# A fused attention and ternary feed-forward layer: the values' scratch in another order, and a prologue with its steps at other places

## The reference

```
qkv = layernorm(x) @ w_qkv;  q, k, v in 16 heads of 32;  q = [q1, q2], k = [k1, k2]
a   = softmax(q1 k1^T / sqrt(32)) - lam * softmax(q2 k2^T / sqrt(32))
lam = exp(lambda_q1 . lambda_k1) - exp(lambda_q2 . lambda_k2) + 0.8
out = a @ v, divided by its rms over the 32 columns, * norm_w * 0.2
x   = x + (heads and rows laid out anew) @ wo
y   = layernorm(x);  h = y @ (ternary(w_fc) * scale)^T + gate * y @ v^T @ fast_b^T @ u^T
x   = x + (relu(h)^2) @ (ternary(w_proj) * scale)^T
```

## Time and profile before

| | |
|---|---|
| median of 3 runs | 3759.39 us |
| profiled execution, its own time | 3755.76 us |
| its span | 3754.0 us |
| PE, DVE, ACT, POOL busy | 99%, 84%, 74%, 16% |
| first score matmul | 101.33 us |
| mean granted clock of TensorE | 0.996 |

### The profile page before, as it was taken

One profiled execution on the slowest core, in us unless ns is written; L12 is line 12 of the kernel. 1 busy time (PEld: TensorE's weight loads), 2 busy tenths in 40 slices (PEclk: granted clock), 3 DMA queues, 4 the chain that ended last, 5 costly groups with the idle time before them and its releaser, 6 DMA issues.

```text
span 3754.0 us, 57605 instructions
## 1 busy us (share of the span) xinstructions
PE 3705.5 (99%) x21704; PEld 2053.0 (55%) x21704; DVE 3152.0 (84%) x2927; ACT 2796.3 (74%) x3629; POOL 584.1 (16%) x269
## 2 busy tenths in 40 slices
PE   7999999999999999999999999999999999999999
PEld 6444444444444444444444444444468888888887
DVE  6899999999999999999999999988865555555554
ACT  4798888888888888888888989888863333333333
POOL 0101101023434343223223201210010000000000
PEclk9999999999999999999999999999999999999999
DMA  7544444445444444554554444534340101010010
GB/s 239 134 102 105 103 105 105 102 100 111 102 99 104 107 106 99 112 115 102 110 114 112 100 100 103 133 82 114 77 152 23 45 23 46 23 46 23 29 40 23
DMA packets 255350, 344.56 MB, mean 92 GB/s; under 512 B 118000, under 2 KB 142576, under 8 KB 254000
## 3 DMA queue, kind: packets, MB, share of 16 engines
q1 hardware_dynamic: 251504, 324.43, 36.6%
q0 software_dynamic: 3392, 15.73, 1.3%
q10 hardware_dynamic: 128, 0.03, 0.0%
HBM read 198.55 MB, written 131.07 MB: 88 GB/s over the span
## 4 chain that ended last, share of the span: by engine, by line
PE 88%; DVE 7%; issue 3%; DMA 1%; ACT 1%; SPq 0%; ACTq 0%; DVEq 0%
PE ps L875 22%; PE ps L850 16%; PE ps L940 13%; PE ps L995 12%; PE ps L786 9%; DVE acc L1632 5%; PE ps L926 4%; PE ps L789 4%; PE ps L896 3%; PE ps L945 2%; PE ps L758 1%; PE ps L1031 1%; PE ps L909 1%; PE ps L1016 1%; ACT pr L1261 0%
## 5 line engine op out<-in xcount | busy, mean ns | idle before, releaser
L1261 ACT ACTIVATE pr<-ps 128x1024 f32<-128x1024 f32 x2048 | 1989.8, 1029 | 257.0 <-PE ps L850 249.5
L1632 DVE TENSOR_TENSOR acc<-acc,pr 128x2048 f32<-128x2048 f32 x768 | 1780.9, 2319 | 40.3 <-ACT pr L1261 10.5
L875 PE MATMUL ps<-pr,vst 128*32 128x512 f32 x8192 | 1010.5, 599 | 0.3 <-DMA vst<-v_scratch 0.3
L850 PE MATMUL ps<-qst,kst 50*128 50x512 f32 x4096 | 781.9, 457 | 9.3 <-ACT pr L1261 6.9
L850 PEld LDWEIGHTS ps<-qst,kst 50*128 50x128 f32 x4096 | 337.1, 184 | 655.1 <-ACT pr L1261 460.1
L875 PEld LDWEIGHTS ps<-pr,vst 128*32 128x32 f32 x8192 | 213.4, 109 | 447.0 <-issue 436.6
L1430 ACT ACTIVATE rb<-ps,scf 128x512 f32<-128x512 f32 x228 | 157.0, 689 | 352.9 <-PE ps L945 352.9
L995 PE MATMUL ps<-tP,hh_ 128*128 128x512 f32 x1024 | 400.3, 391 | 0.6 <-DVE hl_ L1836 0.6
L995 PE MATMUL ps<-tP,hl_ 128*128 128x512 f32 x1024 | 399.5, 390 | 0.0
L786 PE MATMUL ps<-xt,wqh 128*128 128x512 f32 x1024 | 376.8, 419 | 3.0 <-DVE xt L1521 3.0
L940 PE MATMUL ps<-yh,tT 128*128 128x512 f32 x896 | 351.2, 392 | 0.0
(11 more groups left out here) (177 smaller groups left out, 3790.0 us busy)
## 6 DMA issues: line engine op xcount, KB each, us to landing
qst<-q_scratch SPq DMA_DIRECT2D x128, 256.0 KB, 4.6
kst<-k_scratch SPq DMA_DIRECT2D x128, 256.0 KB, 7.0
q_scratch<-stg SPq DMA_DIRECT2D x112, 256.0 KB
k_scratch<-stg SPq DMA_DIRECT2D x112, 256.0 KB
qst<-q_scratch SPq DMA_DIRECT2D x128, 128.0 KB, 4.9
kst<-k_scratch SPq DMA_DIRECT2D x128, 128.0 KB, 7.7
vst<-v_scratch SPq DMA_DIRECT2D x128, 128.0 KB, 4.6
xr<-in_L_attn_x_dram SPq DMA_DIRECT2D x64, 256.0 KB
```

The lines of the kernel that those rows point to most:

```text
L850: ins = e.matmul(ps[:, 2 * c + hh, :], kst[rows, r, j, t * 128:(t + 1) * 128], qst[rows, r, j, c * 512:(c + 1) * 512], start=True, stop=True)
L875: ins = e.matmul(ps[32 * c4:32 * c4 + 32, 4 + j, :], vst[:, r, t, 32 * hh:32 * hh + 32], pr[:, sl, c, hh, :], start=(t == 0), stop=(t == 7 ...
L1261: e.activation(pr[:, sl, c, :, :], ps[:, 2 * c:2 * c + 2, :], ACT.Exp, scale=SCALE).then_inc(s_exp, 1)
L1632: e.tensor_tensor(acc[:, j, :], old, new, ALU.add).then_inc(s_add, 1)
```

## The change

- v_scratch is laid out [2, 128, 8, 8, 64] (row, row tile, pair, columns) instead of [2, 8, 128, 8, 64] (pair first): a store writes 128 rows of 512 numbers, a load reads 4 pieces of 64 numbers for each of 128 partitions.
- w_qkv is split in another order: ScalarE copies columns 0 to 1023 of each k first and the values' columns between its turns; VectorE takes the low part of columns 0 to 127 and 512 to 639 ahead of T = 0, then the values', then the rest. T = 0 and 1 need the first, T = 2 the second, T = 3 the third.
- UNIT_AT is (7, 10, 17, 20) instead of (7, 9, 11, 12). woh is made at T = 16 instead of 22, wol at T = 18 instead of behind the loop. All five statistics steps of chunk 2 stand at T = 14.
- Chunk 2 is issued at T = 8 instead of 10, chunk 3 in pair 0 behind load_qk(1) instead of at T = 22.
- sync_shift(0) is on SyncE ahead of T = 21's store instead of on ScalarE.

```diff
-UNIT_AT = (7, 9, 11, 12)
+UNIT_AT = (7, 10, 17, 20)
-    vsc = nc.dram_tensor("v_scratch", [2, NP, 128, 8, 64], F32, kind="Internal").ap()
+    vsc = nc.dram_tensor("v_scratch", [2, 128, 8, NP, 64], F32, kind="Internal").ap()
...
-            e.dma_start(vsc[b % 2, :, :, t, :].rearrange("q p d -> p q d"),
-                        stage_v(V).rearrange("p (q d) -> p q d", q=NP)).then_inc(s_vsg[V % 2], 16)
+            e.dma_start(vsc[b % 2, :, t].rearrange("p q d -> p (q d)"), stage_v(V)).then_inc(s_vsg[V % 2], 16)
...
-            e.dma_start(vst[:, r, t0:t0 + 4, :], vsc[b % 2, q, :, t0:t0 + 4, :]).then_inc((s_vb if half else s_va)[r], 16)
+            e.dma_start(vst[:, r, t0:t0 + 4, :], vsc[b % 2, :, t0:t0 + 4, q, :]).then_inc((s_vb if half else s_va)[r], 16)
...
             for T in range(24):
+                if T == 21:
+                    sync_shift(e, 0)
                 sync_store(e, T)
...
-                if T in (10, 22):
-                    sync_x(e, 2 if T == 10 else 3)
+                if T == 8:
+                    sync_x(e, 2)
...
                     if d == 0 and P + 1 < NPAIR:
                         sync_load_qk(e, P + 1)
+                    if d == 0 and P == 0:
+                        sync_x(e, 3)
...
-            if n0 == 0 and T == 2:
-                e.wait_ge(s_wl, 8)
+            if n0 == 0 and T in (2, 3):
+                e.wait_ge(s_wl, 4 * T if T == 2 else 12)
...
-                e.activation(wqh[:, k, :], wst[:, k, :], ACT.Copy).then_inc(s_wh, 1)
+                e.activation(wqh[:, k, 0:2 * E], wst[:, k, 0:2 * E], ACT.Copy).then_inc(s_wh, 1)
             for k in range(4):
                 act_turn(e, 0, k, k)
+                e.activation(wqh[:, k, 2 * E:3 * E], wst[:, k, 2 * E:3 * E], ACT.Copy).then_inc(s_wv, 1)
...
-                if T == 21:
-
-                    sync_shift(e, 0)
...
-                if T == 22:
+                if T == 16:
                     e.wait_ge(s_wo, 16)
...
+        def dve_weights(e, k, c0, c1):
+
+            cols = slice(0, 2 * E)
+            src, hi, lo = (t[:, k, cols].rearrange("p (a n) -> p a n", a=2)[:, :, c0:c1] for t in (wst, wqh, wql))
+            e.tensor_tensor(lo, src, hi, ALU.subtract).then_inc(s_wl, 1)
...
-                e.tensor_tensor(wql[:, k, 0:2 * E], wst[:, k, 0:2 * E], wqh[:, k, 0:2 * E], ALU.subtract).then_inc(s_wl, 1)
+                dve_weights(e, k, 0, 128)
                 dve_turn(e, 0, k, k)
             for k in range(4):
+                e.wait_ge(s_wv, k + 1)
                 e.tensor_tensor(wql[:, k, 2 * E:3 * E], wst[:, k, 2 * E:3 * E], wqh[:, k, 2 * E:3 * E], ALU.subtract) \
                     .then_inc(s_wl, 1)
+            for k in range(4):
+                dve_weights(e, k, 128, 512)
...
-                for n in ((0, 1, 2), (3, 4), range(6, 11))[k + 3] if -3 <= k < 0 else ():
+                for n in (((0, 1, 2), (3, 4), range(6, 11)) if T < 12 else (range(5), (), range(6, 11)))[k + 3] if -3 <= k < 0 else ():
                     dve_ln_step(e, C + 1, n)
...
+                if T == 18:
+                    e.wait_ge(s_woh, 1)
+                    e.tensor_tensor(wol[:], wos, woh[:], ALU.subtract).then_inc(s_wol, 1)
```

More of the change, by code:

```diff
@@ L274, in build @@
         s_out = [sem(f"s_out{k}") for k in range(4)]
-        s_pool, s_cst, s_wh, s_wl, s_woh, s_wol, s_lame, s_lamv = (
-            sem(n) for n in ("s_pool", "s_cst", "s_wh", "s_wl", "s_woh", "s_wol", "s_lame", "s_lamv"))
+        s_pool, s_cst, s_wh, s_wv, s_wl, s_woh, s_wol, s_lame, s_lamv = (
+            sem(n) for n in ("s_pool", "s_cst", "s_wh", "s_wv", "s_wl", "s_woh", "s_wol", "s_lame", "s_lamv"))
         s_lnv, s_lna = sem("s_lnv"), sem("s_lna")
@@ L1228, in act_tile @@
                     if Q == 2:
-                        e.wait_ge(s_wl, 8)
+                        e.wait_ge(s_wl, 12)
                     if Q >= STG:
@@ L1775, in vector_program @@
                     dve_shift(e, flag, 0)
-            e.wait_ge(s_woh, 1)
-            e.tensor_tensor(wol[:], wos, woh[:], ALU.subtract).then_inc(s_wol, 1)
             for P in range(NPAIR):
```

## The result

The changed kernel takes 3765.52 us (median of 20 runs, 3762.04 to 3769.03), the kernel before 3757.01 (20 runs, 3753.06 to 3761.64): a ratio of 1.0023, 95% interval 1.0016 to 1.0029. That is slower by 8.5 us, where 2.7 us faster was forecast: 8.8 us above the forecast of 3756.7, and 2.5 above the upper end of the range. The profiled span grows by 8.4 us (3754.0 to 3762.4).

A forecast was written before the change was run, and what follows sets the result against it. The pair loop was taken as bound by TensorE, VectorE leading in pair 0. The first score's gain of 5.1 us, mostly taken back by late chunk 3, left -2.7 us: 3756.7 us, range 3749.5 to 3763.

The forecast's parts named there:

- what decides: Pair 0: the gain at the row sum is what VectorE resumes earlier when chunk 3 lands, -2.7 us.
- R: Start of chunk 3's statistics on VectorE in pair 0: 111.2 instead of 113.87, after a stall of 5 us.
- The half clock: TensorE at T = 22 and 23: half clock after ragged idling, adding 1.9 to 2.7 us; taken at 7 in 10.
- wo at T = 16: ScalarE's copy of wo waits for the second ternary store, landing at 66.8, before the copy's turn at 67.2.
- S: Start of the first score on TensorE: 96.2 instead of 101.33, -5.1 us (94.6 and -6.7 at full clock).
- SyncE's taken alike: Shift rows: four issues take 2.56 us on ScalarE's queue, SyncE's assumed equal; landed at 94 to 96.
- a lag of 5 us still fits: SyncE will have issued T=20's store, its data ready at 83.9, before the shift rows even with this lag.
- Rival C: SyncE lags 5 us or more; first score near 99, chunk 3 lands near 114: 0 to +1, 3759.9; chance 0.10.
- chunk 3's landing: Behind T=23's value store, load_v and eight loads, chunk 3 moves in 2.6 us and lands at 111.2.
- Rival B: Pair 0: the stall for chunk 3 turns TensorE cold, half clock for some 5 us: 3763; chance 0.12.
- Rival A: Chunk 3 does not bind or VectorE makes up the stall: -8.0 to -9.6, so 3750.6; chance 0.25.
- rival D: Values' loads in the pair loop cost TensorE time, 64 x 0.1 to 0.2: +4 to +11, 3766; chance 0.05.

The follow-up runs named there:

- e4: The kernel before with only the values' scratch laid out by rows (layout, store, load): ratio 1.0003 to the kernel before.
- e1: The changed kernel with wo's split late again (woh at T = 22, wol behind the prologue's loop): ratio 1.0026 to the kernel before.
- e10: The changed kernel with the shift rows and chunk 3 at their old places, wo's split kept at T = 16 and 18: ratio 0.9995 to the kernel before.
- e7: The changed kernel with wo's split, the shift rows and chunk 3 all back at their old places: 3752.77 us, ratio 0.9991 to the kernel before.
- e8: The kernel before with only the shift rows moved to SyncE, ahead of T = 21's store: ratio 1.0020 to the kernel before.
- e3: The changed kernel with wo's split late again and chunk 3 back at T = 22: ratio 1.0008 to the kernel before.
- e6: The changed kernel with wo's split and the shift rows back at their old places, chunk 3 still in pair 0: ratio 1.0020 to the kernel before.
- e9: The kernel before with only chunk 3's load moved to pair 0, behind load_qk(1): ratio 1.0029 to the kernel before.
- e12: e11 with UNIT_AT = (7, 10, 13, 15): ratio 1.0001 to the kernel before.
- e2: The changed kernel with only chunk 3's load back at T = 22 on SyncE: ratio 1.0012 to the kernel before.
- e11: e7 with chunk 3 issued on ScalarE's queue behind the shift rows: ratio 1.0001 to the kernel before.

## Why the prediction was wrong

**Right: what decides.** That the gain is what VectorE resumes earlier in pair 0, and that nothing behind it gives anything back. R moved by +9.5, the row sum by +9.55, the span by +8.4. The sign was wrong because R was: not 2.7 earlier but 9.5 later.

**Right: the early steps.** T = 0's copy at 20.36 (said: 20.1), the gap for chunk 2 1.87 (said: 1.9), values by rows at nothing (e4). The half clock came in T = 22 (granted 0.50 from 95 to 100) and cost 2.9 us (8.4 from the flag to the end of T = 23, instead of 5.5), a little over the 1.9 to 2.7 that I gave it. The end of T = 23 in e1 (95.96, said: 95.5) is close in part by luck: my figure had the split of wo in it and 3.6 us of stall in T = 21, e1 has neither the split there nor more than 2.45 of stall.

**Wrong, and first in time: wo at T = 16.** I had the second ternary store issued at 58.5 and landing in 8.3, "66.8, against 67.2": covered by 0.4 us. It left at 61.41, because SyncE was late itself, and took 14.65. The two stalls in T = 21 became 5.96 and 1.49 instead of 1.5 and 2.1, VectorE's flag step came at 93.98 instead of 87.5, and T = 23 ended 7 us late. In the changed kernel this wait is on the chain that sets both S and chunk 3's place; removing it alone wins nothing (e1), because SyncE is as late. Once the other two are undone it is 1.8 us of R in one pair of traces (e10 against e7), which isn't clear of the spread.

**Wrong, and decisive for the first score: "SyncE's taken alike", "a lag of 5 us still fits".** I priced four issues by those of ScalarE and the landing by the same rows, on a queue that held nothing else (the page of before lists 128 packets for it in all; after, that queue is gone). SyncE had T = 18 to 20's stores of 512 KB each ahead of them. In the changed kernel S came at 105.59 (said: 96.2), 9.4 late: 6.5 of it is the late flag step, since the issues began 2.2 behind it, about as priced (at 96.17, said: 87.5 + 2.1), and 2.7 the landing, 6.7 behind the end of the issue instead of 4.0. VectorE was then ready for chunk 3 12.7 behind S, where I had put about 10. Without the late flag SyncE's lag takes its place: in e1 the issues began at 95.93, 7.8 behind the flag step (88.11). In the five kernels with the rows on SyncE they landed 6.2 to 8.4 us behind the end of the issue, and in e8, where nothing else is moved, S came 9.2 later than in the kernel before. Rival C named the lag, but gave it +1 us at most, because I let it end at the shift rows: all that stands behind them on SyncE moves as well.

**Wrong, and decisive for R: chunk 3's landing.** Forecast 111.2, measured 123.4, 12.2 later. By the terms of the prediction: T = 23's values issued at 103.53 instead of 96.15 (+7.4), landing in 4.52 instead of 3.5 (+1.0), load and eight loads in 4.3 instead of 5.0 (-0.7), chunk 3 in 11.1 instead of 6.5 (+4.6). The last term alone would have turned -2.7 into a loss. My 6.5 let chunk 3 move at about 400 GB/s as soon as the eight loads were through; the loads ran at 160 to 190 GB/s from 110 to 120, and the stretch from 120 to 125, with chunk 3 in it, at 291. The rows of before had both prices in them: the chunk's own 9.46 to land, and the maximum of 11.9 for a values' store. I took medians over the whole execution, most of whose DMAs meet a share of 0.48, for a stretch whose share is 0.92 and more. The first term is T = 23's late end in the changed kernel (102.87, its values copied by 103.5), and SyncE's lag where T = 23 ends early: in e1 and e3, where it ended at 96, its values left at 106.09 and 104.00. And an early issue would not have helped: in e6 they left at 98.67 and took 10.92 us to land. The landing that I put at 99.7 was at 107.8 to 110.2 in all five kernels with chunk 3 behind load_qk(1).

**Rival B** was the mechanism nearest to the result: chunk 3 landing past 114, 3763. It had too small a chance, 0.12, and its price (3763, measured 3765.5) is near by luck: it was made of 1.1 for chunk 3 and 2.5 or more for a cold TensorE, where chunk 3 cost 9.5 and the cold nothing. TensorE does idle for 4.36 us ahead of 130.1 and then runs at half clock (granted 0.50 from 130 to 134), the sign that the prediction gave for B. But VectorE's late start alone explains the row sum: 15.4 us from R to the row sum before, 15.4 after. In e6, where TensorE idled for 11.03 us and ran at half clock until 137, it was 16.4: that is what the cold cost at its worst here, 1.0 us. Rival A (chunk 3 doesn't bind) and rival D (the values' loads cost TensorE time in the loop) did not occur.

## What to carry to other kernels

Price a DMA by its neighbours in the queue and in time, not by a median over the kernel: in a stretch with other DMAs ahead of it, read the longest landings. Before a small transfer on which an engine stands is moved to a queue with bulk stores, or a load behind another's landing, write out what is ahead of it and what is behind it; an engine's queue that lags takes every later item along. And where undoing one edit wins nothing, undo them in pairs: two paths that end alike hide each other.

## What the runs showed of the hardware

- **Small DMAs landed sooner from a queue that held nothing else.** Four shift-row DMAs landed 4.0 to 4.3 us behind the end of their issue from ScalarE in the five kernels where TensorE waited for them (before, e4, e9, e10, e12), and 6.2 to 8.4 behind it from SyncE (after, e1, e2, e3, e8), where they kept TensorE waiting 9.8 to 12.3 us in e8, e1 and e3. The Trainium skill, DMA: Bandwidth & Descriptors, Issuing engines are not separate DMA queues, says that DMAs of all issuers run on the same 16 engines and interleave, and that several issuers save only the time of the issue. For a megabyte e11 agrees, as the second queue won the kernel nothing. For the four small DMAs e8 doesn't: beside 4.1 us for the lag and length of the issue, the landing itself took 3.3 us more, and here the measurement decides. That they pass what the other queue holds is the likely reason; no run shows the order within a queue.
- **Landing times in the prologue are far from the medians:** 14.65 us for a ternary store, 14.86 for a k_scratch store (e11), 9.0 to 12.9 for chunk 3 (1 MB), where the shortest landing of a chunk in the changed kernel is 5.6; a values' store takes 2.4 at the median and 13.1 at most. Full DMA engines are not the whole reason: the ternary store was under way from 61 to 76 us, at shares of 0.53 to 0.70. What else holds a landing back is not shown.
- **An issue can hold its engine for microseconds:** the same four issues took 2.56 to 4.05 us on ScalarE (before, e7) and 2.72 to 5.62 on SyncE (after, e1), and the one issue of chunk 3 held SyncE for 4.81 us in the kernel before and for 0.42 in the changed one. Why is not shown; a full queue would do it.
- **256-byte pieces in a load cost almost nothing here:** a 128 KB load lands in 4.8 us at the median (after and e4) instead of 4.6.
